# Router logits in four 32-column strips of TensorE, turned by VectorE, with all queues in a new order

## The reference

```
x = x + 0.5 * quantized_matmul(layernorm(x))      # int8 quantized 128 x 128 product
x = x + recurrent_block(layernorm(x))             # rmsnorm, conv of 4 taps, gates, scan, gated FFN of 512
x = x + 0.5 * quantized_matmul(layernorm(x))
x = x + 0.5 * moe(layernorm(x))                   # 8 routed experts, the best 2, and a shared one
x = x + linear_attention(layernorm(x))
x = x + 0.5 * moe(layernorm(x))
```

```
logits = einsum('bsh,eh->bse', x, Wr) + rb        # Wr is 8 x 128, rb has 8 entries
probs = sigmoid(logits)
scores, idx = top_k(probs, 2)
cw = (one_hot(idx, 8) * scores[..., None]).sum(-2)
out = shared(x) + sum_e cw[..., e] * expert_e(x)  # silu(x Wg') * (x Wu') Wd', inner size 256
```

## Time and profile before

| what | us |
|---|---|
| median of three runs | 701.86 |
| lowest and highest run | 701.73, 702.95 |
| profiled execution: span from first to last instruction | 703.3 |
| TensorE matmul busy | 616.8 |
| TensorE weight loads busy (beside the matmuls) | 487.0 |
| VectorE busy | 487.2 |
| ScalarE busy | 398.0 |
| GpSimd busy | 387.9 |

### The profile page before, as it was taken

How to read it: one execution, slowest core, us unless ns; L and a number is a source line. 1 busy time by engine, 2 the same in 40 slices (tenths; PEclk the granted TensorE clock), 3 DMA queues, 4 the chain that set the end, 5 groups by cost and what they waited for, 6 DMA issues and landing times.

```text
span 703.3 us, 14597 instructions
## 1 busy us (share of the span) xinstructions
PE 616.8 (88%) x4232; PEld 487.0 (69%) x4232; DVE 487.2 (69%) x1730; ACT 398.0 (57%) x1036; POOL 387.9 (55%) x416
## 2 busy tenths in 40 slices
PE   1478999999799989899986998899999999987971
PEld 1234565566566888788885886779878998776970
DVE  6986777878889867554625996878865874546334
ACT  3477887999686454554445556464665446343530
POOL 4425434435747787767653413651865764766642
PEclk9699999999999999999999999999999999999996
DMA  7998000000042366577668010214324545566886
GB/s 263 410 411 342 1 0 1 1 1 20 31 107 61 95 179 179 168 214 223 189 200 286 22 66 11 63 46 117 89 73 134 157 115 161 166 197 175 251 302 214
DMA packets 60126, 100.99 MB, mean 144 GB/s; under 512 B 10288, under 2 KB 28592, under 8 KB 59792
## 3 DMA queue, kind: packets, MB, share of 16 engines
q1 hardware_dynamic: 50832, 81.52, 37.7%
q0 software_dynamic: 8640, 17.84, 7.1%
q10 hardware_dynamic: 576, 0.69, 0.3%
HBM read 61.79 MB, written 38.23 MB: 142 GB/s over the span
## 4 chain that ended last, share of the span: by engine, by line
PE 59%; DVE 10%; ACT 9%; issue 7%; DMA 6%; POOL 5%; SPq 4%; POOLq 0%; ACTq 0%; DVEq 0%
PE bank L1071 14%; PE bank L1048 7%; PE bank L1282 4%; PE bank L934 3%; DMA tin<-rows_by_expert 3%; PE bank L959 3%; PE bank L308 3%; PE bank L945 3%; PE bank L510 3%; PE bank L663 3%; PE bank L313 3%; POOL rows_by_expert L830 2%; PE bank L677 2%; PE bank L1054 2%; PE bank L692 2%
## 5 line engine op out<-in xcount | busy, mean ns | idle before, releaser
L830 POOL DMA_INDIRECT rows_by_expert<-xx,sidx x128 | 126.3, 987 | 71.7 <-DVE xx L809 35.8
L1071 PE MATMUL bank<-tint,twt 128*128 128x128 f32 x1136 | 150.7, 278 | 10.9 <-DVE thidt L1109 5.7
L1071 PEld LDWEIGHTS bank<-tint,twt 128*128 128x128 f32 x1136 | 138.6, 192 | 26.3 <-issue 13.6
L1109 DVE TENSOR_TENSOR thidt<-tsil,bank 128x256 f32<-128x256 f32 x142 | 58.9, 419 | 98.6 <-ACT tsil L1087 86.6
L1120 POOL DMA_INDIRECT rows_done<-tout,tin x98 | 95.4, 974 | 52.4 <-ACT tout L1095 28.3
L1087 ACT ACTIVATE tsil<-bank 128x256 f32<-128x256 f32 x142 | 54.4, 384 | 82.1 <-PE bank L1071 80.4
L1048 PE MATMUL bank<-e_dn,thidt 128*128 x568 | 89.8, 283 | 7.3 <-issue 3.5
L1048 PEld LDWEIGHTS bank<-e_dn,thidt 128*128 128x128 f32 x568 | 76.4, 193 | 19.4 <-issue 18.8
L1095 ACT ACTIVATE tout<-bank,tin 128x128 f32<-128x128 f32 x142 | 51.5, 367 | 35.1 <-PE bank L1054 33.7
L1120 POOL DMA_INDIRECT rows_done<-tout,tdst x44 | 43.8, 996 | 30.1 <-issue 11.8
L1080 ACT ACTIVATE tint<-bank 128x128 f32<-128x128 f32 x142 | 38.2, 275 | 37.1 <-PE bank L1054 36.8
(11 more groups left out here) (271 smaller groups left out, 1363.9 us busy)
## 6 DMA issues: line engine op xcount, KB each, us to landing
twt<-moe_gu SPq DMA_DIRECT2D x142, 256.0 KB
rows_by_expert<-tout SPq DMA_DIRECT2D x25, 715.0 KB, 19.6
tin<-rows_by_expert SPq DMA_DIRECT2D x142, 65.0 KB
hid<-rows_done SPq DMA_DIRECT2D x12, 512.0 KB, 4.8
x<-x_in SPq DMA_DIRECT2D x8, 256.0 KB, 4.1
rows_by_expert<-xx,sidx POOLq DMA_INDIRECT x128
out<-x SPq DMA_DIRECT2D x8, 256.0 KB, 3.5
rows_done<-tout,tin POOLq DMA_INDIRECT x98, 3.0
```

The costliest lines, as they stand in the source:

```text
L830: pool.indirect_dma_start(out=rows_by_expert, out_offset=bass.IndirectOffsetOnAxis(ap=sidx[h][:, k:k + 1], axis=0), in_=xx[h][:, r, t, :], ...
L1071: m = pe.matmul(bank[UP_BANKS[p][j]][:, c * P:(c + 1) * P], weights[:, c * P:(c + 1) * P], tint[g % TURNS][:, :], start=True, stop=True)
L1109: dve.tensor_tensor(thidt[g % TURNS][:, :, :].rearrange("p j c -> p (j c)"), tsil[g % TURNS][:, :], bank[UP_BANKS[p][j]][:, INNER:2 * INNE ...
```

## The change

The router's weight becomes the stationary operand: `w_r` is widened from 8 to 32 columns, the last 24 of them zero, and used in four products. Product b takes the tokens with row 32b to 32b+31 of each of the four tiles (128 moving columns) and writes PSUM partitions 32b to 32b+31, that is, one of four strips of 32 output columns of TensorE. The logits so stand with experts on the partitions of a strip. The bias goes into the tanh as ScalarE's per-partition bias (`half_rb`, made once at the start), so the step `r_bias_vector` is gone; the tanh now reads 128 x 128 out of PSUM. Then VectorE turns each 32 x 32 block (`r_strips_vector`), which puts tokens back on the partitions, and `r_rank_vector` reads 8 of every 32 columns. The strips and their turned form lie in the first and second half of the `above` buffer.

```diff
-        w_r = sb("w_r", [P, E_ROUTED])
+        w_r = sb("w_r", [P, STRIP])
+        strips = [above[h].rearrange("p t e j -> p (t e j)")[:, 0:P] for h in range(2)]
+        turned = [above[h].rearrange("p t e j -> p (t e j)")[:, P:2 * P] for h in range(2)]
         def r_logits_tensor(pe, u, p):
             pe.wait_ge(s_rxt, n(u, p))
-            tile_mm(pe, bank[R_BANK], xtr[u % 2], w_r[:, :], E_ROUTED).then_inc(s_rl, 1)
-
-        def r_bias_vector(dve, u, p):
-            dve.wait_ge(s_rl, n(u, p))
-            dve.tensor_tensor(probs[u % 2][:, :, :],
-                              bank[R_BANK][:, 0:TILES * E_ROUTED].rearrange("p (t e) -> p t e", t=TILES),
-                              rows[:, None, R_RB:R_RB + E_ROUTED].to_broadcast([P, TILES, E_ROUTED]),
-                              ALU.add).then_inc(s_rlb, 1)
+            if n(u, p) == 1:
+                pe.wait_ge(s_pool_const, 1)
+            blocks = xtr[u % 2][:, :].rearrange("p (t b r) -> p b t r", t=TILES, r=STRIP)
+            for b in range(P // STRIP):
+                m = pe.matmul(bank[R_BANK][b * STRIP:(b + 1) * STRIP, 0:P], w_r[:, :], blocks[:, b, :, :],
+                              start=True, stop=True)
+            m.then_inc(s_rl, 1)
 
         def r_tanh_scalar(act, u, p):
-            act.wait_ge(s_rlb, n(u, p))
-            act.activation(probs[u % 2][:, :, :], probs[u % 2][:, :, :], ACT.Tanh, scale=0.5).then_inc(s_pr, 1)
+            if n(u, p) == 1:
+                act.wait_ge(s_const, 4)
+            act.wait_ge(s_rl, n(u, p))
+            if n(u, p) > 2:
+                act.wait_ge(s_first2, n(u, p) - 2)
+            act.activation(strips[u % 2], bank[R_BANK][:, 0:P], ACT.Tanh, scale=0.5,
+                           bias=half_rb[:, :]).then_inc(s_pr, 1)
+
+        def r_strips_vector(dve, u, p):
+            dve.wait_ge(s_pr, n(u, p))
+            dve.transpose(turned[u % 2], strips[u % 2]).then_inc(s_rlb, 1)
 
         def r_rank_vector(dve, u, p):
-            dve.wait_ge(s_pr, n(u, p))
-            dve_step(dve, dve.tensor_scalar(probs[h][:, :, :], probs[h][:, :, :], 0.5, 0.5, ALU.mult, ALU.add))
+            dve.wait_ge(s_rlb, n(u, p))
+            dve_step(dve, dve.tensor_scalar(probs[h][:, :, :], turned[h].rearrange("p (t e) -> p t e", t=TILES)[:, :, 0:E_ROUTED], 0.5, 0.5, ALU.mult, ALU.add))
...
+        def k_strips_vector(dve):
+            dve.wait_ge(s_first, 16 * FIRST)
+            dve_step(dve, dve.memset(rb_wide[:, :], 0.0))
+            dve_step(dve, dve.tensor_scalar(rb_wide[:, 0:E_ROUTED], rows[:, R_RB:R_RB + E_ROUTED], 0.5, None, ALU.mult))
+            dve_step(dve, dve.transpose(rb_turned[:, :], rb_wide[:, :]))
+            dve.tensor_copy(half_rb[:, :], rb_turned[:, 0:1]).then_inc(s_const, 1)
...
-            sp_.dma_start(w_r[:, :], moe_r).then_inc(s_load, 16)
+            sp_.dma_start(w_r[:, 0:E_ROUTED], moe_r).then_inc(s_load, 16)
         def k_first_gpsimd(pool):
+            pool.memset(w_r[:, E_ROUTED:STRIP], 0.0)
...
         @block.sync
         def _(sp_):
             k_loads_sync(sp_)
+            for j in range(0, 3):
+                t_load_sync(sp_, 0, j)
             for j in range(0, 2):
+                t_weights_sync(sp_, 0, j)
+            for j in range(3, 7):
                 t_load_sync(sp_, 0, j)
...
```

More of the change, by code:

```diff
@@ L30 @@
 TOP_K = 2
+STRIP = 32
 NT = TOP_K * TOKENS // P + E_ROUTED - 1
@@ L1569, in _ @@
+            t_weights_sync(sp_, 0, 45)
+            t_load_sync(sp_, 0, 47)
+            for j in range(46, 49):
+                t_weights_sync(sp_, 0, j)
+            for j in range(48, 53):
+                t_load_sync(sp_, 0, j)
+            t_weights_sync(sp_, 0, 49)
+            t_load_sync(sp_, 0, 53)
+            for j in range(50, 53):
                 t_weights_sync(sp_, 0, j)
@@ L1719, in _ @@
-            t_weights_sync(sp_, 1, 62)
-            for j in range(64, 66):
+            for j in range(64, 67):
                 t_load_sync(sp_, 1, j)
@@ L2844, in _ @@
[L2844 to L2855 removed]
+            x_up_tensor(pe, 0, 25)
+            for j in range(27, 29):
+                x_io_tensor(pe, 0, j)
@@ L3511, in _ @@
             x_silu_scalar(act, 0, 12)
             x_out_scalar(act, 0, 11)
+            x_silu_scalar(act, 0, 13)
+            for j in range(16, 18):
+                x_in_scalar(act, 0, j)
+            x_out_scalar(act, 0, 12)
+            e_silu_scalar(act, 4, 0, 1)
+            for j in range(14, 17):
+                x_silu_scalar(act, 0, j)
+            x_in_scalar(act, 0, 18)
+            x_out_scalar(act, 0, 13)
+            x_in_scalar(act, 0, 19)
+            x_silu_scalar(act, 0, 17)
@@ L3637, in _ @@
             x_in_scalar(act, 0, 52)
-            for j in range(49, 51):
+            for j in range(48, 51):
                 x_silu_scalar(act, 0, j)
+            e_silu_scalar(act, 7, 0, 1)
+            x_silu_scalar(act, 0, 51)
             x_out_scalar(act, 0, 48)
@@ L3727, in _ @@
+            for j in range(69, 71):
+                x_out_scalar(act, 0, j)
             r_apply_scalar(act, 0, 1)
@@ L3882, in _ @@
-            x_out_scalar(act, 1, 20)
+            for j in range(12, 14):
+                x_out_scalar(act, 1, j)
+            for j in range(18, 20):
+                x_in_scalar(act, 1, j)
+            x_silu_scalar(act, 1, 17)
+            for j in range(14, 16):
+                x_out_scalar(act, 1, j)
+            x_in_scalar(act, 1, 20)
+            for j in range(18, 20):
+                x_silu_scalar(act, 1, j)
+            x_in_scalar(act, 1, 21)
+            e_silu_scalar(act, 5, 1, 0)
@@ new lines, in _ @@
+            x_out_scalar(act, 1, 16)
+            x_in_scalar(act, 1, 22)
+            x_out_scalar(act, 1, 17)
+            x_silu_scalar(act, 1, 20)
+            g_late_scalar(act, 6, 4)
+            g_late_scalar(act, 6, 5)
+            x_silu_scalar(act, 1, 21)
+            g_late_scalar(act, 6, 6)
+            g_late_scalar(act, 7, 4)
+            x_in_scalar(act, 1, 23)
+            x_silu_scalar(act, 1, 22)
+            g_cross_scalar(act, 6)
+            x_in_scalar(act, 1, 24)
+            for j in range(18, 20):
+                x_out_scalar(act, 1, j)
@@ L3888, in _ @@
             x_in_scalar(act, 1, 26)
-            x_silu_scalar(act, 1, 25)
+            for j in range(25, 27):
+                x_silu_scalar(act, 1, j)
             x_in_scalar(act, 1, 27)
@@ new lines, in _ @@
+            for j in range(49, 52):
+                x_out_scalar(act, 1, j)
+            for j in range(52, 55):
+                x_silu_scalar(act, 1, j)
+            x_in_scalar(act, 1, 56)
+            x_silu_scalar(act, 1, 55)
+            x_in_scalar(act, 1, 57)
+            for j in range(52, 54):
+                x_out_scalar(act, 1, j)
+            for j in range(58, 60):
+                x_in_scalar(act, 1, j)
+            x_out_scalar(act, 1, 54)
+            x_silu_scalar(act, 1, 56)
@@ L4002, in _ @@
+            x_in_scalar(act, 1, 60)
+            x_silu_scalar(act, 1, 57)
+            for j in range(55, 57):
+                x_out_scalar(act, 1, j)
             x_in_scalar(act, 1, 61)
```

2654 lines of the change are left out of this document (1243 added, 1411 removed).

## The result

| | median us | lowest to highest | runs |
|---|---|---|---|
| before | 702.40 | 701.73 to 708.17 | 4 |
| changed | 716.22 | 710.45 to 717.71 | 4 |

The changed kernel takes 1.0156 of the time of before (95% interval 1.0098 to 1.0214). By the medians it takes 13.8 us more; the ratio is not that of the medians, and by it the difference is 11 us. 698.3 us was predicted, with a range of 689 to 706.5: wrong in sign and outside the range. Beside experiments on two other chips the ratio was 1.0105 (1.0048 to 1.0163) and 1.0127 (1.0062 to 1.0192), and the medians were 8.2 and 9.3 us apart, so 8 to 14 us is what there is to explain.

The account below looks back on a forecast made before the run. TensorE was taken as the bound from 75 to 350 and 400 to 640 us; logits -1.5, table loads -1.8, start -0.8, constants +0.5 make -3.6 from 703.3, so 699.7, or 698.3 us for the median; range 689 to 706.5.

Parts of the forecast that it names:

- The rest of the order: Other moved steps, such as unit 1's router and the shared expert's last product: slack or a wait covers them, zero.
- (b): Logits groups: switch costs on both sides, strips in turn; 706.2 us likelier, 709.5 upper; chance 0.25, including an order that stalls.
- (c): TensorE gets shorter but GpSimd's scatters and tile loads set the end, or new waits cancel the gain; 701.9 us, chance 0.15.
- slower: The outcome that the changed kernel takes longer than before; chance 0.25, the same as the switch-cost and stalling-order rival.
- The logits term: Sixteen logits groups on TensorE: each 0.71 us instead of 0.81, saving 1.6 us, of which 1.5 us reaches the end.
- rival (a): Logits groups: strips fully side by side, no wait at the switch; saves 8.9 us, median 690.9 us; chance 0.18.
- 95% of it, the busy share of the two stretches: TensorE, 75 to 350 and 400 to 640 us: that share of the logits' 1.6 us saving reaches the end, 1.5 us.
- Router chain: VectorE's turn replaces the bias step, 0 to +2.5 us; ScalarE's tanh grows 0.8 us; TensorE's work covers it, counted nothing.
- the five table loads: ScalarE: 31 loads instead of 36, 6.4 us less work, of which 1.8 us was counted at the end.
- The start: ScalarE's copy ahead of an exponential, -0.8 us; VectorE's constants near 55 us, +0.5; the -1.8 is fewer ScalarE table loads.

Follow-up runs that it names:

- The second half of that order: Strips with the order of before up to about 240 us and the changed kernel's order behind it: 719.27 us, 1.0161 of before.
- strips alone: Kernel before with the logits in strips, its order kept: 709.18 us, 1.0023 of before; 0.9885 where before takes 818.33 us.
- the halves: Strips with the new order only to 240 us, 705.54 us, or only from 240 us, 719.27 us; before took 706.29 us on that chip.
- its two runs: Changed kernel with SyncE's list as in before, 713.06 us, 1.0083 of before; with weights moved ahead on SyncE, 711.45 us, 1.0085.
- the order alone: The changed kernel's order with the logits, bias and tanh of before: 837.50 us, 1.0223 of before, where before takes 818.33 us.

## Why the prediction was wrong

**The failed step is "The rest of the order".** It looked at two of the moved steps, found 17 us of slack behind one and a wait at the end over the other, and wrote "nothing" and "Zero" for the whole rest. The second half of that order costs 10.1 us (719.27 against 709.18). None of the places where the trace shows it waiting was looked at, such as the quantization ahead of unit 4's ranking, or weights behind loads on SyncE. How much each of them costs stays open. The rivals named it twice in half a sentence, in (b) as "an order that stalls somewhere" and in (c) as one that "gives back in new waits", with no place and no price. Its chance stood in "slower", 0.25, its size was outside the range.

**The logits term.** A group takes 0.45 us of TensorE with its way in, not 0.71. The eight passes of four strips do run side by side, as rival (a) had it: they take 0.27 us of it (0.16 us to the start of the last pass, and 0.11 us until a next one could follow), where the prediction had 5 steps, 0.54 us. The switches cost 0.18 us in all, where the prediction had 0.17 and rival (a) nothing; that it put the whole on the way back, and the trace half on either side, changes no sum. The page "TensorE: Matmul & The Clock Gate", section "Part 3: Packing small matmuls", of the Trainium skill says such products run concurrently; the trace agrees. The page "TensorEngine Tiling (Array Packing)", section "Key Properties", of the Trainium skill has a change of mode drain the engine; the trace agrees, with some 0.09 us for each of the two changes.

**From the engine to the end.** 16 x 0.36 us is 5.8 us on TensorE, and strips alone took 709.18 us against 706.29. The step "95% of it, the busy share of the two stretches" failed on that chip. A busy share of 96% is the time in which some pass is in flight, and each lasts 278 ns at a pace of 112 ns; it does not say that the next pass had been waiting. The window of strips alone shows it: fewer busy us, the same passes.

**Router chain.** The turn, 306 ns, is in the 0.2 to 0.35 us foretold. The tanh grew by 139 ns, not 47. ScalarE's busy time fell by 1.0 us, not 6: the five table loads went (6.4 us), and the tanh took back 2.2; the rest was not traced. Nothing was counted for the scaling behind the turn, and it cost 2.9 us more in all (6.3 for 3.4 us), nearly all of it through two single ones of 1.08 and 2.21 us that ran beside GpSimd's 128x512 instructions.

**The start.** Foretold -0.8, -1.8 and +0.5 us up to 240 us; the root came 3.3 us and the first tile 6.3 us earlier. The direction was right and the size too small; on the chip of the halves 3.6 us of it reached the end, by the medians, which is not clear of the noise.

**What stays open.** Of the 10.1 us, some 2 may belong to the order on SyncE, which neither of its two runs shows clear of the noise. The rest was not divided: the traces show waits of 1 to 2.5 us on TensorE for rows, for VectorE's `thidt` and for the ranking, some with a stretch at half clock behind them. Whether GpSimd's rate would set the end if they were gone, and why the first pair differed by 13.8 us and later ones by 8 to 9, was not shown; 3 to 4 us of the latter may be the half clock, which the first trace of the changed kernel has twice as often in the tile stage as the later ones (mean clock 0.93 and 0.97; estimate). Nor was the order alone run where before takes 702 to 706 us.

## What to carry to other kernels

When a change comes with a new order, the order is the change: compare the two orders at each stage where an engine runs without a gap, and give it a range of both signs before pricing the edit itself. A high busy share does not make an engine the bound. An engine whose instructions follow each other at a fixed spacing, here GpSimd's DMAs at 1.26 us, is one to test, which was not done here. In a queue that waits in order, what is needed first must not stand behind what another engine releases late, and the right place for it is a property of the whole order, not a rule.

## What was unexpected in the hardware

- A VectorE instruction on 32 columns took 2.21 us instead of 0.18 beside two 128x512 additions of GpSimd, and ended with them; in all three traces of the changed kernel, and not where the additions were moved. The page "SBUF — State Buffer", section "SBUF: two separate sides", of the Trainium skill says that the two engines share a pair of ports under an exclusive lock, on which the loser is blocked for the whole instruction; the trace agrees, except that one small instruction was blocked here over two large ones. That the ports were the cause was not tested by itself.
- Eight fp32 passes of 128 columns in four strips of 32 hold TensorE for 0.36 us, where eight of 8 columns on the whole array hold it for 0.81. These follow one another at 0.10 us, nearly the 0.11 us of passes of 128 columns, so the streaming does not set their pace; the load of 128 columns (192 ns, that of 32 takes 108) is the likely one, which no run varied alone.
- Going from the whole array into the strips and back cost some 0.09 us each time.
- Some waits of about 2 us in the tile stage of the changed kernel were followed by a stretch at 1.2 GHz in which TensorE was busy again, so that such a wait cost nearly twice its length: all four in the first trace, two of three and two of four in the later ones. The wait of 2.07 us of before had none.
- The same kernel took 702 to 706 us on some chips and 818 to 822 on others. For the strips in the old order, with 706.1 and 808.8 us, nearly all of the difference arose between the first and the last tile of each of the two blocks (44 and 52 us).
